# Scores in 64-row halves of the TensorE array, and a value product over two chunks, in a chain of seven attentions

## The reference

```python
def attention(x, ctx, wq, wk, wv, wo, bo, heads):
    q, k, v = split_heads(x @ wq), split_heads(ctx @ wk), split_heads(ctx @ wv)
    a = softmax(einsum('bhid,bhjd->bhij', q, k) * dh ** -0.5)
    return merge_heads(einsum('bhij,bhjd->bhid', a, v)) @ wo + bo

x = x + cross(x, ctx)                         # unit 0: 20 heads of 8, 512 keys
x = x + self(ln(x)); x = x + cross(ln(x), ctx); x = x + geglu_ff(ln(x))   # units 1 and 2
# unit 3: 8 heads of 20, 508 context rows; unit 4: 96 query rows against the 256 rows of x
x = x + self(ln(x)); x = x + cross(ln(x), ctx); x = x + geglu_ff(ln(x))   # units 5 and 6
```

## Time and profile before

| | us |
|---|---|
| median of 3 runs | 1082.69 (1079.75 to 1086.96) |
| the profiled execution | 1083.78 |
| its span, first to last instruction | 1082.0 |
| mean granted TensorE clock | 0.981 of full |

### The profile page before, as it was taken

How to read it: one execution, slowest core, us unless ns; L and a number is a source line. 1 busy time by engine, 2 the same in 40 slices (tenths; PEclk the granted TensorE clock), 3 DMA queues, 4 the chain that set the end, 5 groups by cost and what they waited for, 6 DMA issues and landing times.

```text
span 1082.0 us, 21250 instructions
## 1 busy us (share of the span) xinstructions
PE 1034.7 (96%) x7808; PEld 719.5 (67%) x7808; DVE 689.4 (64%) x1603; ACT 675.4 (62%) x1400; POOL 74.0 (7%) x129
## 2 busy tenths in 40 slices
PE   8999989999998999999998998999999899999978
PEld 5656666667685666767685666676768566765646
DVE  3777757875546567875755775787555556777631
ACT  4556666766664666766765665776665556766641
POOL 3000000000002100001010000000100110000000
PEclk9899999999999999999999999999999999999995
DMA  8110001110232101010113010101021400111000
GB/s 195 42 39 17 21 22 44 30 31 11 49 77 56 25 21 45 21 31 22 35 31 89 21 26 20 45 21 31 10 60 30 103 20 22 34 25 40 11 7 7
DMA packets 31150, 40.26 MB, mean 37 GB/s; under 512 B 10324, under 2 KB 22232, under 8 KB 30728
## 3 DMA queue, kind: packets, MB, share of 16 engines
q1 hardware_dynamic: 31048, 38.89, 14.9%
HBM read 10.97 MB, written 0.66 MB: 11 GB/s over the span
## 4 chain that ended last, share of the span: by engine, by line
PE 87%; DVE 5%; ACT 4%; issue 3%; DMA 0%; POOLq 0%; POOL 0%; DVEq 0%; ACTq 0%
PE st_ps L775 18%; PE pv_ps L831 17%; PE mx_ps L794 17%; PE sp_ps L757 8%; PE sp_ps L758 7%; PE sp_ps L876 4%; PE sp_ps L858 3%; DVE mx L1221 2%; PE sp_ps L808 2%; PE sp_ps L950 2%; PE sp_ps L938 2%; PE sp_ps L989 2%; ACT probs L1062 2%; ACT oT L1069 1%; PE sp_ps L893 1%
## 5 line engine op out<-in xcount | busy, mean ns | idle before, releaser
L1221 DVE TENSOR_REDUCE mx<-mx_ps 128x1 f32<-128x512 f32 (+2 forms) x720 | 475.4, 685 | 184.4 <-PE mx_ps L794 181.1
L1062 ACT ACTIVATE probs<-st_ps 128x512 f32<-128x512 f32 x720 | 400.6, 597 | 184.3 <-PE st_ps L775 178.4
L794 PE MATMUL mx_ps<-ring,qT 128*128 128x512 f32 (+2 forms) x864 | 294.9, 400 | 6.9 <-issue 3.8
L775 PE MATMUL st_ps<-qT,ring 128*128 128x256 f32 (+1 forms) x1408 | 276.1, 298 | 5.4 <-ACT probs L1062 3.2
L775 PEld LDWEIGHTS st_ps<-qT,ring 128*128 128x128 f32 (+1 forms) x1408 | 217.8, 190 | 80.4 <-ACT probs L1062 40.6
L831 PE MATMUL pv_ps<-probs,v 128*9 128x256 f32 (+3 forms) x2944 | 223.8, 377 | 3.0 <-ACT probs L1062 2.3
L794 PEld LDWEIGHTS mx_ps<-ring,qT 128*128 128x128 f32 x864 | 143.5, 190 | 88.9 <-DVE mx L1221 45.7
L831 PEld LDWEIGHTS pv_ps<-probs,v 128*9 128x9 f32 (+2 forms) x2944 | 44.9, 90 | 64.3 <-issue 19.2
L1111 ACT ACTIVATE kdense<-sp_ps 128x512 f32<-128x512 f32 (+2 forms) x116 | 57.4, 539 | 24.4 <-PE sp_ps L876 23.9
L1049 ACT ACTIVATE ks<-sp_ps 128x320 fp32r<-128x320 f32 x80 | 35.2, 440 | 42.3 <-PE sp_ps L858 27.5
L876 PE MATMUL sp_ps<-identr,ks 128*128 128x128 f32 (+1 forms) x416 | 59.7, 279 | 0.7 <-DVE qs L1187 0.6
(11 more groups left out here) (134 smaller groups left out, 1050.2 us busy)
## 6 DMA issues: line engine op xcount, KB each, us to landing
ring<-kdense SPq DMA_DIRECT2D x256, 64.0 KB, 2.0
wb<-in_w_blk SPq DMA_DIRECT2D x4, 1400.0 KB, 9.1
ring<-kdense SPq DMA_DIRECT2D x160, 32.0 KB, 1.8
ring<-kdense SPq DMA_DIRECT2D x32, 127.0 KB, 2.3
wd<-in_w_down SPq DMA_DIRECT2D x4, 400.0 KB, 9.5
ring<-oT SPq DMA_DIRECT2D x16, 64.0 KB, 3.2
ctx_n<-in_ctx SPq DMA_DIRECT2D x4, 192.0 KB, 6.6
x<-in_x SPq DMA_DIRECT2D x4, 160.0 KB, 3.3
```

Source lines behind the costliest of these rows:

```text
L775: mm = pe.matmul(st_ps[s % N_ST][0:kr, i * a["nq"]:(i + 1) * a["nq"]], key_op(n, h)[:, c * P:c * P + kr], query_op(u, b)[:, h // of(u), :] ...
L794: mm = pe.matmul(mx_ps[o % N_MX][0:rows, j * a["nk"]:(j + 1) * a["nk"]], query_op(u, b)[:, h // of(u), tt * P:tt * P + rows], key_op(n, h) ...
L1062: nc.scalar.activation(probs[0:kr, s % N_P, 0:w], st_ps[s % N_ST][0:kr, 0:w], ACT.Exp, scale=float(a["dh"]) ** -0.5).then_inc(S["probs_rea ...
L1221: nc.vector.tensor_reduce(mx[b][0:rows, t, heads[0]:heads[-1] + 1], mx_ps[(o - 1) % N_MX][0:rows, 0:a["hpm"] * a["nk"]].rearrange("p (h k) ...
```

## The change

Four things change together.

- **Halves.** The keys stay dense (`kdense`, `kca`), and it is the queries that are spread: each `q_tr` of units with heads of 8 is followed by a step `qdma`, four DMAs from `qT` to `qpad`, in which each 64-row half holds one head and zeros. A score matmul then reads 64 rows: `side(u, h)` gives rows 0 to 63 or 64 to 127. A slot holds two heads of the same half; slots alternate between the halves, and maximum items are dealt in the opposite order (`same_half`, `items_of`). Unit 4 has two heads a slot in place of four, so there are 736 slots.
- **Maximum rows.** `negm` writes its eight rows of a quad into a small tile `mn`; one matmul transposes it, VectorE copies 72 rows to `mT`, and a step `mdma` puts the rows in their places among the queries: eight DMAs of two rows x 128 columns for a quad with heads of 8, four for one of unit 3, two for unit 4. The first slot of a quad waits for them.
- **Value product.** A `pv` step takes two chunks (`RUN` = 2) in place of one: 184 steps in place of 368, of sixteen instructions each. `N_P` goes from 6 to 10.
- **Planner.** It knows three shapes of TensorE work (64 rows, 32 columns, full), books `MODE` = 95 ns for a change of shape, and lets the halves run side by side. `kdma`, `clear`, `m_zero` and the ring are gone.

```diff
+def half(u, h):
+    return h % of(u) // (of(u) // 2)
+def same_half(u, qd):
+    hs = range(4 * qd, 4 * qd + 4)
+    return [[h for h in hs if half(u, h) == k] for k in range(2)]
+def runs(u):
+    n_c = -(-ATT[u]["nk"] // P)
+    return [list(range(c, min(c + RUN, n_c))) for c in range(0, n_c, RUN)]
+def items_of(u, qd):
+    a, tiles = ATT[u], q_tiles(u)
+    per = [[(t, rows, hs[i:i + a["hpm"]]) for i in range(0, 2, a["hpm"]) for t, rows in tiles] for hs in same_half(u, qd)]
+    return [item for both in zip(per[1], per[0]) for item in both]
...
-    if kind == "kdma":
-        return 0, [("dma", 2600)]
+    if kind in ("qdma", "mdma"):
+        return 0, [("dma", 400)]
...
     if kind == "max":
         rows = a["hpm"] * nk
-        return 4 + 0.417 * rows, [("dve", 60 + 1.05 * rows)]
+        return 4 + 0.45 * rows, [("dve", 60 + 1.05 * rows)]
...
-        return TR * groups * len(q_tiles(u)), dve(groups * nq)
+        return TR, dve(P)
     if kind == "st":
-        return 218, act(512)
+        return 236, act(512)
     if kind == "pv":
-        return 4 * nq * 0.47, []
+        return len(runs(u)[step[2]]) * nq * 1.57, []
...
+    def pe_free(step):
+        if shape(step) != mode:
+            return max(lanes) + MODE
+        return max(clock["pe"], max(lanes) if mode != "rows" else lanes[lane(step)])
...
-        done[step] = t + (DMA_LATENCY if step[0] == "kdma" else HANDOFF)
+        done[step] = t + (DMA_LATENCY if step[0] in ("qdma", "mdma") else HANDOFF)
...
+        def key_op(u, b, h):
+            g = h // of(u)
+            if u == 4:
+                return (kca[b][:, g, :] if g < 2 else kdense[b][:, 4, (g - 2) * SQ:(g - 1) * SQ])[side(u, h), :]
+            return kdense[b][side(u, h), g, :]
+        def query_op(u, b, h):
+            g = h // of(u)
+            if ATT[u]["sr"] == 32:
+                return qpad[b][side(u, h), h % 2, g, :]
+            return (qTc if u == 4 else qT)[b][side(u, h), g, :]
...
-                    if step[0] == "kdma":
...
+                    if step[0] == "qdma":
+                        _, u, b, gg = step
+                        g0, g1 = 2 * gg, min(2 * gg + 2, 5)
+                        taken(sp, ("q_tr", u, b, gg))
+                        for j in range(4):
+                            rows = slice(32 * j, 32 * j + 32)
+                            sp.dma_start(qpad[b][rows, j % 2, g0:g1, :].bitcast(F32),
+                                         qT[b][rows, g0:g1, :].bitcast(F32)).then_inc(qpad_in[b % 2][gg], 16)
+                    elif step[0] == "mdma":
...
+                        taken(sp, ("mtr", n))
+                        for i, (t, rows) in enumerate(q_tiles(u)):
+                            for j in range(k):
+                                src = mT[n % 2][64 * i + j:64 * i + 8:k, 0:rows].bitcast(F32)
+                                at = slice(sr * j + 3 * dh, sr * j + 3 * dh + 2)
+                                if sr == 32:
+                                    dst = qpad[b][at, j % 2, qd, i * P:i * P + rows].bitcast(F32)
+                                else:
+                                    dst = query_dst(u, b)[at, 2 * qd:2 * qd + 2, i * P:i * P + rows].bitcast(F32)
+                                sp.dma_start(dst, src).then_inc(m_in[n % 2], 16)
...
                         if s == quads[n]["start"]:
-                            taken(pe, ("mtr", n))
+                            pe.wait_ge(m_in[n % 2], m_landed[n])
...
-                                           key_op(n, h)[:, c * P:c * P + kr], query_op(u, b)[:, h // of(u), :],
-                                           start=True, stop=True)
+                                           key_op(u, b, h)[:, c * P:c * P + kr], query_op(u, b, h), start=True, stop=True)
...
-                        gs = range(4 * qd // of(u), (4 * qd + 4) // of(u))
-                        for k, g in enumerate(gs):
-                            for i, (t, rows) in enumerate(q_tiles(u)):
-                                mm = pe.matmul(bank[:, k * a["nq"] + i * P:k * a["nq"] + i * P + rows],
-                                               query_stack(u, b)[0:rows, t, g * of(u):(g + 1) * of(u), :].rearrange("p h s -> p (h s)"),
-                                               identr[0:rows, 0:rows], start=True, stop=True)
-                        mm.then_inc(full, 1)
+                        rows = q_tiles(u)[0][1]
+                        pe.matmul(bank[0:72, 0:rows], mn[n % 2][0:rows, :, :].rearrange("p t m -> p (t m)")[:, 0:72],
+                                  identr[0:rows, 0:rows], start=True, stop=True).then_inc(full, 1)
...
-                        mine = [s for s in quads[n]["slots"] if slots[s]["c"] == c]
+                        mine = [s for s in quads[n]["slots"] if slots[s]["c"] in runs(u)[k]]
```

More of the change, by code:

```diff
@@ L399, in simulate, with lane, shape @@
     clock = dict(pe=0, act=0, dve=0, pool=0, dma=0)
+    mode, lanes = "full", [0, 0]
+    def lane(step):
+        if step[0] == "st":
+            return half(slots[step[1]]["u"], slots[step[1]]["heads"][0])
+        if step[0] == "max":
+            return half(quads[step[1]]["u"], quads[step[1]]["items"][step[2]][2][0])
+        return None
+    def shape(step):
+        return "rows" if step[0] in ("st", "max") else "columns" if step[0] == "pv" else "full"
+    def pe_free(step):
+        if shape(step) != mode:
+            return max(lanes) + MODE
+        return max(clock["pe"], max(lanes) if mode != "rows" else lanes[lane(step)])
     done, order, uses, maxes = {}, [], [], []
@@ L425, in simulate @@
                 start = max(start, done[maxes[-N_MX]])
-            key = (max(start, clock["pe"]), due.get(step)) if cost(step, quads)[0] else (max(start, clock["pe"]), (-10**6, 0, 0))
+            key = (max(start, pe_free(step)), due.get(step)) if cost(step, quads)[0] else (max(start, clock["pe"]), (-10**6, 0, 0))
             if best is None or key < best[0]:
@@ L458, with operands @@
 LOW = {"kv_proj", "qkv_proj", "q_proj", "ca_q"}
+def operands(q):
+    u, b, qd = q["u"], q["b"], q["qd"]
+    gg = qd // 2 if ATT[u]["sr"] == 32 else qd
+    pairs = 2 if ATT[u]["nk"] > SQ else 1
+    query = ("q_tr", 4, b, 0) if u == 4 else ("qdma" if ATT[u]["sr"] == 32 else "q_tr", u, b, gg)
+    return [("k_tr", u, b, pr, gg) for pr in range(pairs)] + [query]
 SIGNALS = {
@@ L608, in build @@
                 for s in quads[step[1]]["slots"]:
-                    if slots[s]["c"] == step[2]:
+                    if slots[s]["c"] in runs(quads[step[1]]["u"])[step[2]]:
                         if slots[s]["last"]:
```

237 lines of the change are left out of this document (110 added, 127 removed).

## The result

| | before | after |
|---|---|---|
| median, us | 1083.8 (1079.8 to 1087.0, 4 runs) | 1481.8 (1472.4 to 1514.2, 4 runs) |
| the profiled execution | 1083.8 | 1472.4 |
| ratio | | 1.365, 95% interval 1.355 to 1.374 |
| span of the profiled execution | 1082.0 | 1470.6 |
| mean granted TensorE clock | 0.981 | 0.721 |

The kernel is 398 us slower; 1020 was forecast. Some executions of a kernel run over 1.5% longer than its fastest, at a lower granted clock (here the one of 1514.2): the ratios leave them out, the medians don't.

What follows compares the result with a forecast made beforehand. TensorE, busy 96% of the span, was taken to bound the kernel. Its terms, -103 - 55 + 76 - 15 = -97 us, with +30 for the queues and +5 at the start, took 1082 to 1020 us; range 930 to 1115.

Steps and rivals of the forecast that it cites:

- Term (1): Score and maximum matmuls on TensorE: 64-row halves overlap and save 30% of 344 us, -103 us.
- nothing gained, or half: Bounds on the gain from score and maximum matmuls in halves on TensorE: none, or -172 us.
- Term (3): Borders between 64-row score work and 128-row sp_ps work on TensorE: 380 changes of shape at 0.20 us, +76 us.
- Term (2): Value steps on TensorE: 184 over two chunks instead of 368, saving 0.30 us of overhead each, -55 us.
- Term (4): Transposes of the maximum rows on TensorE: 116 left of 248, at 0.11 us each, -15 us.
- The queues: Maximum-row DMAs on SP's queue: TensorE stalls 0.3 us a quad at the first slot, +30 us.
- rival C: First slot of each quad: waiting for the rows' trip, up to 3.3 us by 100, gives 1140 us; chance 0.15.
- the cover: The lead of the maximum over a quad's slots, taken to hide the rows' trip but for 0.3 us a quad.
- Starts within 10 ns: Sign of overlap: score and maximum matmuls in opposite halves start within some 10 ns of each other.
- Under 280 us of start-to-start time: Sign of overlap: score and maximum matmuls together take under 280 us instead of some 344.
- Fewer than 400 borders: Sign on TensorE: fewer than 400 borders between scores and sp_ps, a first matmul 0.2 us late at each.
- Wait over 100 us, then C: Sign at the scores: if their wait for a DMA exceeds 100 us, rival C is right.

Runs made afterwards that it cites:

- before_halves: The kernel before, own order, with score and maximum matmuls of units with heads of 8 reading only their head's 64 rows: 1183.5 us, ratio 1.088.
- clock_parts: The kernel before with back-to-back bursts of matmuls (128 rows, opposite halves, one half, column tiles) in front; 400 in opposite halves took 24.25 us.
- no_trip: The changed kernel, same order, without the 848 DMAs of the maximum rows and with the exponential's scale cut to 0.01: 1211.8 us.
- no_trip_full: The changed kernel without the maximum-row DMAs, same order, and with score and maximum matmuls of all 128 rows: 1109.6 us, ratio 1.025.
- before_max_half: The kernel before with only the maximum matmuls (heads of 8) in 64 rows and scores in 128: 1254.8 us, ratio 1.150.
- clock_return: The kernel before with eight bursts of matmuls in front, one kind each, each behind a pause of 8.7 us; one half took 85.7 us.
- half+full: A burst ahead of the kernel before: 75 rounds of 4 matmuls of 64 rows and 2 of 128x128 by 128 columns; 134.6 us.
- full+full: A burst ahead of the kernel before: 75 rounds of 4 matmuls of 128 rows and 2 of 128x128 by 128 columns; 1.28 us a round.
- the swapped order: The kernel before with 64-row score and maximum matmuls (heads of 8), a quad's maximum items dealt in the opposite order of halves: ratio 1.105.
- four_dmas: The changed kernel with maximum rows in four DMAs a quad in place of eight and SP's real costs in the planner: 1249.4 us.

## Why the prediction was wrong, step by step

**The clock, which no term of the sum had.** The prediction worked at full clock throughout and named a clock that falls because of pauses at the quads only as what would make it wrong. That is the step that failed most. By the table, after was low for 821 us and before for 43, so the clock would be up to (821 - 43) / 2 = 389 us, all of the difference between the two profiled executions. But TensorE stood idle for 103 us of the low time after and for 5 before, which a full clock would not shorten; that leaves up to 340. At full clock after would take at least 1060, and about 1110 if these waits stay, so the forecast of 1020 would still have missed by 40 to 90. The trip and the halves both lower the clock: it falls 50 times with the trip, 21 without it, 10 with 128 rows besides, and 4 in the kernel before. The bursts show one way in which the halves do it, since work in one half doesn't bring a low clock back. That they also add falls is shown (11 for 4 in before_halves, with the same stalls), but not how.

**Term (1), halves, -103 us: right mechanism, wrong sign in the sum.** The halves overlap fully (clock_parts). At full clock in the order of before, overlap and changes cancel (before_halves, 120 to 185 us). With the clock it is +98 us there, and +86 in the order of after (no_trip less no_trip_full). The floors of these two (1003 and 1071) differ by 68 us the other way: that would be the gain at full clock, changes of shape paid, if the low stretches held streaming alone. Forecast were 103 - 76 = 27. The step that failed is "nothing gained, or half": a bound from below should have been open for the clock. The estimate of 1.54 for two row tiles, from the Trainium skill (TensorE: Matmul & The Clock Gate, Measured speedup vs the span model), was too low for dense work: 2.00 was measured.

**Term (3), 380 changes at 0.20 us, +76: about right, the number too low and the price too high.** There are 478 borders between the score work and sp_ps (521 before), so the planner grouped less than supposed. The price shows where the kernel before and before_halves do the same five steps at full clock:

```profile
448.11 0.50 PE L794 MATMUL mx_ps<-ring,qT 128*128 128x512 f32 x1
448.45 0.56 PE L876 MATMUL sp_ps<-identr,ks 128*128 128x128 f32 x4
448.84 0.45 PE L775 MATMUL st_ps<-qT,ring 128*128 128x256 f32 x2
449.13 0.56 PE L876 MATMUL sp_ps<-identr,ks 128*128 128x128 f32 x4
449.53 0.45 PE L794 MATMUL mx_ps<-ring,qT 128*128 128x512 f32 x1
```
```profile
499.01 0.50 PE L799 MATMUL mx_ps<-ring,qT 64*128 64x512 f32 x1
499.44 0.66 PE L881 MATMUL sp_ps<-identr,ks 128*128 128x128 f32 x4
500.03 0.51 PE L780 MATMUL st_ps<-qT,ring 64*128 64x256 f32 x2
500.46 0.66 PE L881 MATMUL sp_ps<-identr,ks 128*128 128x128 f32 x4
501.05 0.50 PE L799 MATMUL mx_ps<-ring,qT 64*128 64x512 f32 x1
```

From the first start to the last it is 1.42 us without a change of shape and 2.04 with four, 0.155 each; the quickest tenth of the borders from scores to sp_ps, 0.117 us before and 0.205 in before_halves, has only the 0.09 going in, and the rest is at the second transpose and on the way back. before_max_half agrees from afar: its floor is 102 us above that of before for 759 changes between 64 and 128 rows (those into and out of value steps not counted), 0.13 each. So 478 changes are some 62 to 74 us at full clock. The Trainium skill (TensorEngine Tiling (Array Packing), Key Properties) names the drain alone; here more than the 0.09 at the border was paid. In the low clock it is more: in clock_return a round of half+full takes 1.77 us and one of full+full 1.28, 0.24 a change.

**Term (2), value steps, -55 us.** 179 runs of value work were left for 361, as said, and one of 16 instructions takes 0.98 us in no_trip, start to start, where two of eight took 1.10 (206.03 to 206.58, twice, in the earlier trace rows). But alone on the kernel before it costs 42 us. The start-to-start time of value work went from 210 to 183 us, so 27 were gained inside the value work (the 0.09 ahead of a step and the 0.10 behind it lie outside this count), and more than that given back, by waits for ScalarE and VectorE and by the clock. The prediction had seen that the earlier trace rows won't shrink; it had not costed that these waits grow with steps of twice the length. That the length is the reason (the two engines running dry, and filling up behind it) is argued, not shown.

**Term (4), transposes, -15 us.** 116 transposes of 72 rows are left, and the copy to mT takes 0.28 us for the 0.26 estimated. Not measured alone; no_trip_full holds it and is 26 us slower than the kernel before all the same, which the 42 us of (2) would explain.

**The queues, +30 us.** The mechanism of rival C, with its place, is there in full: issues 0.6 us apart, up to 5.8 us of wait at the first slot, 116 us of TensorE's matmuls standing in 65 places (139 us before weight loads, mostly the same ones). It was given 0.15. The mean over 100 quads is 1.2 us, beyond its point of decision of 1.0. The step that failed here is the cover: the estimate of 0.3 came from waits of the kernel before, whose order was laid out for a copy of 0.4 us at this place, while the new order leaves the 2.6 us that its planner believes in for a trip of 6.4. Rival C's price, 1140 us, was too low as well, since it had no clock in it either: the trip costs 279 us, of which 124 are idle time of TensorE and 154 are busy time, longer for the same instructions. The clock can be at most (821 - 378) / 2 = 222 us of it, or 181 without the idle time in the low stretches.

**What would show each step.** Starts within 10 ns: true, in no_trip's timeline a maximum and a score start together:

```profile
510.23 0.50 PE L871 MATMUL mx_ps<-kdense,qpad 64*128 64x512 f32 x1
510.23 0.61 PE L851 MATMUL st_ps<-qpad,kdense 64*128 64x256 f32 x3
```

Under 280 us of start-to-start time: at low clock not to be read. Fewer than 400 borders: no, 478. Wait over 100 us, then C: it was, 116.

**Open.** Why work in one half doesn't bring the clock back, what makes the clock fall while TensorE is busy, and why the swapped order has fewer but longer low stretches. No version here beats the kernel before: what is best of the change, without its trip, has a floor of 1003 us at full clock (no_trip), and doesn't get that clock.

## What to carry to other kernels

Before work is cut into row tiles, look at the granted clock and at what there is to bring it back: in bursts, one half of the array held a full clock but didn't regain it, and in these kernels' mix 64-row work came with more falls and longer low stretches (before_halves: 11, of 23 us in the mean; the kernel before: 4, of 11 us). Where a planner's costs make the order, a cost that is wrong by a factor of twelve (0.4 for 4.8 us of issue) puts a stall at every place where the order trusts it; put the measured issue time of each DMA in first. And a coarser step on the longest engine should be tried alone: here it saved 27 us of value work and cost 42.

## What the runs showed of the hardware

- Work in one 64-row half, without a pause, stays at 1.2 GHz for 85.7 us if it starts there, and stays at 2.4 GHz for 24.25 us if it starts there (clock_return, clock_parts). Both halves side by side, 128 rows, or four column tiles have full clock 3 to 6 us into the burst.
- In a mix of 64-row, 32-column and 128-row work the clock also fell from full to half with no idle time of TensorE ahead: busy 7.20 us of 7.20 at 1.00, then 13.70 of 13.70 at 0.50 (before_halves, 499 to 520 us).
- Two row halves overlap completely: 400 matmuls in 24.25 us, the time of 200 in one half (clock_parts).
- A change between 64 and 128 rows costs 0.13 to 0.16 us at full clock (before_max_half, before_halves) and 0.24 at half (clock_return), measured start to start.
- A DMA of two rows from SBUF to SBUF (qpad<-mT) costs SP 563 ns of issue, 0.60 us start to start, whether the rows have 128 columns (after) or 256 (four_dmas).
